# Sums and rounding passes of the ternary weights: in blocks early on, or in twelve steps spread over the head of the program

## The reference

```python
x = _layernorm(x + attn(x))            # 16 heads on 4 KV heads, rotary, ALiBi, softmax
x = _layernorm(x + xattn(x, ctx))      # 16 heads of 16, windows of 64, masks by cell
x = _layernorm(x + ffn(x))

def _weight_quant(w):                  # w_gate, w_up, w_down: 1024 x 256, 1024 x 256, 256 x 1024
    scale = 1.0 / jnp.clip(jnp.mean(jnp.abs(w)), 1e-05)
    return jnp.clip(jnp.round(w * scale), -1.0, 1.0) / scale
gate = silu(bitlinear(x, w_gate)); up = bitlinear(x, w_up)
ffn = bitlinear(gate * up, w_down)     # activations rounded to 8 bits per token
```

## Time and profile before

| | before |
|---|---|
| median of 3 runs | 2233.26 us (2232.71 to 2235.64) |
| the profiled execution | 2231.77 us |
| its span, first to last instruction | 2230.0 us |
| mean granted TensorE clock | 0.999 |
| PE busy | 2155.6 us, 97% |
| DVE busy | 1950.3 us, 87% |
| ACT busy | 1704.1 us, 76% |
| POOL busy | 1424.6 us, 64% |

### The profile page before, as it was taken

The page is one execution under the profiler, slowest core; times in us unless marked ns, Lnnn a source line. Parts: engine busy times, 40 slices in busy tenths (PEclk is TensorE's granted clock), DMA queues, the critical chain, the costliest instruction groups (busy, mean ns, idle before and its releaser), DMA issues. The chain is left out here.

```text
span 2230.0 us, 58875 instructions
## 1 busy us (share of the span) xinstructions
PE 2155.6 (97%) x19819; PEld 1671.1 (75%) x19819; DVE 1950.3 (87%) x7968; ACT 1704.1 (76%) x4754; POOL 1424.6 (64%) x1678
## 2 busy tenths in 40 slices
PE   7899999999999999999999999999999999999987
PEld 6677777777787777777777777777777777777755
DVE  5779988999988899998899998889999888999874
ACT  4687778887778888777888777788877788887743
POOL 2566766666776666776666677666667666667631
PEclk9999999999999999999999999999999999999999
DMA  4010111111110110111111111111011101101100
GB/s 164 11 34 25 37 27 33 28 35 28 36 37 23 34 31 25 37 37 30 30 28 36 26 37 37 25 35 28 25 37 37 38 23 28 37 25 37 32 16 10
DMA packets 85400, 74.69 MB, mean 33 GB/s; under 512 B 18544, under 2 KB 79344, under 8 KB 85104
## 3 DMA queue, kind: packets, MB, share of 16 engines
q1 hardware_dynamic: 85104, 70.93, 11.9%
HBM read 45.72 MB, written 8.39 MB: 24 GB/s over the span
## 5 line engine op out<-in xcount | busy, mean ns | idle before, releaser
L1404 POOL TENSOR_TENSOR prob<-prob,precs 128x512 f32<-128x512 f32 x512 | 528.8, 1040 | 561.8 <-DVE precs L1017 557.6
L1312 ACT ACTIVATE prob<-prob,nmax 128x256 f32<-128x256 f32 x1024 | 509.0, 505 | 45.1 <-DVE nmax L1010 45.1
L1010 DVE CUSTOM_DVE_ANT_0 prob<-bank,alibi 128x256 f32<-128x256 f32 x1024 | 371.2, 418 | 23.4 <-PE bank L728 23.1
L1319 ACT COPY pT<-bank 128x512 f32<-128x512 f32 x512 | 303.4, 593 | 55.8 <-PE bank L617 55.5
L617 PE MATMUL bank<-ident,prob 128*128 128x128 f32 x2048 | 316.6, 277 | 4.0 <-ACT pT L1319 3.0
L1336 ACT ACTIVATE px<-px,nmx 128x128 f32<-128x128 f32 x1024 | 313.9, 400 | 4.8 <-DVE nmx L1119 4.8
L617 PEld LDWEIGHTS bank<-ident,prob 128*128 128x128 f32 x2048 | 231.3, 141 | 56.5 <-issue 38.1
L747 PE MATMUL bank<-pT,v_sb 128*64 128x256 f32 x2048 | 249.8, 386 | 3.4 <-DVE qq_lo L1001 3.1
L1119 DVE CUSTOM_DVE_ANT_0 px<-bank,mask 128x128 f32<-128x128 f32 x1024 | 226.3, 286 | 4.8 <-PE bank L807 3.0
L747 PEld LDWEIGHTS bank<-pT,v_sb 128*64 128x64 f32 x2048 | 136.2, 136 | 100.9 <-issue 39.3
L1312 ACT ACTIVATION_READ_ACCUMULATOR prob<-prob,nmax 128x1 f32 x1024 | 199.5, 195 | 0.0
(11 more groups left out here) (216 smaller groups left out, 6028.9 us busy)
## 6 DMA issues: line engine op xcount, KB each, us to landing
raw<-in_xT SPq DMA_DIRECT2D x32, 256.0 KB, 2.9
xtok<-in_x SPq DMA_DIRECT2D x32, 256.0 KB, 2.9
kx_tok<-in_ctx SPq DMA_DIRECT2D x32, 256.0 KB, 3.0
raw<-in_ctxT SPq DMA_DIRECT2D x32, 256.0 KB, 2.9
kx<-k_sin SPq DMA_DIRECT2D x256, 32.0 KB, 2.0
vs<-vx SPq DMA_DIRECT2D x64, 128.0 KB, 2.3
out_y<-x SPq DMA_DIRECT2D x32, 256.0 KB, 3.1
cellk<-in_cell SPq DMA_DIRECT2D x32, 64.0 KB, 3.8
```

The costliest lines, as they stand in the source:

```text
L1010: v.tensor_tensor_reduce(out=prob[:, (2 * p + q) % SLOTS, c, :], in0=psum[SCORES[c]][:, q * L:(q + 1) * L], in1=alibi[:, p % 2, :], scale= ...
L1312: nc.scalar.activation(prob[:, (2 * p + q) % SLOTS, c, :], prob[:, (2 * p + q) % SLOTS, c, :], ACT.Exp, bias=nmax[:, i:i + 1], scale=-1.0, ...
L1319: nc.scalar.copy(pT[:, p % 2, :, :, q * P:(q + 1) * P].rearrange("p c k n -> p (c k) n"), bank[:].rearrange("p (c n) -> p c n", c=4)).then ...
L1404: g.tensor_tensor(prob[:, n % SLOTS, :, :], prob[:, n % SLOTS, :, :], precs[:, 2 * n:2 * n + 2].unsqueeze(2).to_broadcast([P, 2, L]), ALU. ...
```

## The change

The instructions and their operands stay the same. They move in the lists of `HEAD`. The sums become a step kind of their own, `sum` m on ACT, and the passes a kind `ternary` m, i on DVE, one pass each. The twelve steps stand between steps of batches 0 and 1. The matmul ("prep", 5) moves on PE from behind the last `Q` of batch 0 to behind `S` 6 of batch 0, the mean ("prep", 6) on DVE to the same place. `kx_clear` on POOL moves from between `R` 5 and 6 to between `R` 13 and 14. PE loses 26 fillers, 7 of another 15, and 8 of another 14. A pass waits for the one before it at its start, and only the last of each matrix still waits for its own end. The steps ("prep", 6 to 8) on ACT, which are waits alone, move later, and so does ("prep", 8) on PE. `BODY`, `TAIL` and SP's list are unchanged.

```diff
     "dve": [
-        (0, 'qT', 1), (0, 'Q', 0, 2), (0, 'prep', 6), (0, 'Q', 1, 2), (0, 'S', 2), (0, 'prep', 7), (0, 'qT', 2),
+        (0, 'W', 0), (0, 'ternary', 0, 0), (0, 'R', 12), (0, 'R', 13), (1, 'qT', 0), (0, 'ternary', 0, 1), (0, 'S', 7),
+        (0, 'ternary', 0, 2), (0, 'mask'), (0, 'R', 14), (0, 'R', 15), (0, 'O', 2), (0, 'ternary', 1, 0), (1, 'kT'),
+        (1, 'S', 0), (0, 'ternary', 1, 1), (1, 'qT', 1), (0, 'ternary', 1, 2), (1, 'R', 0), (1, 'R', 1), (1, 'Q', 0, 2),
+        (1, 'S', 1), (0, 'ternary', 2, 0), (1, 'R', 2), (0, 'O', 3), (0, 'ternary', 2, 1), (1, 'S', 2), (0, 'ternary', 2, 2),
...
                     dve.wait_ge(pre_dve, P_CROSSED + 4)
-                    ternary(0)
-                elif n > 6:
-                    ternary(n - 6)
-
-            def ternary(m):
-                done = P_CROSSED + 4 + 3 * m
-                v.tensor_scalar(stage[m], stage[m], wrec[:, m:m + 1], MAGIC, ALU.mult, ALU.add).then_inc(pre_dve, 1)
-                dve.wait_ge(pre_dve, done + 1)
-                v.tensor_scalar(stage[m], stage[m], MAGIC, 1.0, ALU.subtract, ALU.min).then_inc(pre_dve, 1)
-                dve.wait_ge(pre_dve, done + 2)
-                v.tensor_scalar((wg16, wu16, wd16)[m][:].rearrange("p k n -> p (k n)"), stage[m], -1.0, None, ALU.max).then_inc(pre_dve, 1)
-                dve.wait_ge(pre_dve, done + 3)
+
+            def ternary(m, i):
+
+                dve.wait_ge(pre_dve, P_CROSSED + 4 + 3 * m + i)
+                if i == 0:
+                    v.tensor_scalar(stage[m], stage[m], wrec[:, m:m + 1], MAGIC, ALU.mult, ALU.add).then_inc(pre_dve, 1)
+                elif i == 1:
+                    v.tensor_scalar(stage[m], stage[m], MAGIC, 1.0, ALU.subtract, ALU.min).then_inc(pre_dve, 1)
+                else:
+                    v.tensor_scalar((wg16, wu16, wd16)[m][:].rearrange("p k n -> p (k n)"), stage[m], -1.0, None, ALU.max).then_inc(pre_dve, 1)
+                    dve.wait_ge(pre_dve, P_CROSSED + 4 + 3 * m + 3)
...
-                        elif args[0] == 5:
-
-                            act.wait_ge(later_loaded[2], 16 * len(later_loads[2]))
-                            act.wait_ge(wo_split, 2)
-                            for m in range(3):
-                                if m > 0:
-                                    act.wait_ge(w_sums, m)
-                                nc.scalar.activation(kx[:].rearrange("p k h n -> p (k h n)"), stage[m], ACT.Abs, accum_out=wsum[:, m:m + 1])\
-                                    .then_inc(w_sums, 1)
+                    elif kind == "sum":
+
+                        m, = args
+                        act.wait_ge(later_loaded[2], 16 * len(later_loads[2]))
+                        act.wait_ge(wo_split, 2)
+                        if m > 0:
+                            act.wait_ge(w_sums, m)
+                        nc.scalar.activation(kx[:].rearrange("p k h n -> p (k h n)"), stage[m], ACT.Abs, accum_out=wsum[:, m:m + 1]).then_inc(w_sums, 1)
```

## The result

| | before | after |
|---|---|---|
| median | 2233.45 us of 7 runs (2232.71 to 2235.64) | 2244.13 us of 7 runs (2239.83 to 2244.99) |
| the profiled execution, its span | 2231.77, 2230.0 us | 2244.49, 2242.7 us |
| mean granted TensorE clock there | 0.999 | 0.995 |

The ratio is 1.0046, 95% interval 1.0037 to 1.0056: 10.7 us slower. The forecast had the sign, but only half of the size, and the time lies outside its range (up to 2242.5).

What follows compares the result with a forecast made beforehand. PE bounds the kernel, busy 97%, with DVE's list binding in the head. 3.0 us earlier, then 7.7 later, gives 4.75 late; plus 0.7 for clock and 1.5 from profile to median: 2238.7 us, range 2231.5 to 2242.5.

Steps and rivals of the forecast that it cites:

- Part 1: Head up to W 0 of batch 0: passes and sums moved away make it 3.0 us earlier.
- Part 2: From W 0 of batch 0 to qT 2 of batch 1: 7.7 us lost, leaving qT 2 4.75 us late.
- the walk through DVE's list: Stepping through DVE's list from 89 us, nine passes of 1.23 us plus POOL waits: qT 2 of batch 1 4.75 us late.
- the wrong branch: Pass 3 near 95 us gets in ahead of POOL's memsets, ending at 96.05; losing to them would cost another 1.2 us.
- The clock: PE waits 2 us ahead of kT and 3.3 ahead of V of batch 1; a drop costs 0.7 us, at most 1.7.
- Neither stretch can take up a delay: PE from 117 us, and 140 to 165 us where ACT is busy, have no room to absorb lateness.
- a constant shift to the end: From qT 2 of batch 1, near 120 us, lateness stays the same through the rest of the execution.
- the dense part: The stretch where PE waits for next to nothing, from about 186 us, so head gains or losses carry through.
- The 41 fillers cost nothing, apart from the clock: The removed PE fillers in the head stood in waits, so removing them changes no time except through the clock.
- The passes fit: Rival, chance 0.32: passes lose nothing to POOL in part 2; 1.2 us late, 2234.5 us, no difference.
- the lead survives: Rival, chance 0.11: the 3.0 us lead reaches qT 2 of batch 1, kT at 95.5 or earlier; 2228.8 to 2230.3 us.
- Memsets and clock both go wrong: Rival, chance 0.14: pass 3 waits for both memsets, clock falls at kT and V; 7.7 us, 2241.0 us.

Runs made afterwards that it cites:

- e8_again: The changed kernel run once more, unedited: 2242.68 us, ratio to before 1.0047.
- e4_sums_back: The changed kernel with the three sums, their matmul with its 26 fillers, and the mean back in their old places, passes still spread: 2239.78 us, ratio 1.0032.
- e14: e10 without the 12 fillers ahead of SX 0 of batch 0: 2243.23 us, ratio to before 1.0049.
- e10: The changed kernel with fillers in every PE wait over 1.5 us up to 150 us, 271 in the head: 2240.90 us, ratio to before 1.0036.
- e16: e10 with 33 more fillers in PE's waits, 304 in the head: 2237.70 us, ratio to before 1.0024.
- e13: e10 with the kx memsets moved behind R 15 and 14 fillers ahead of kT: 2243.25 us, ratio to before 1.0045.
- e12: The kernel before with only the change's removal of 41 fillers: 2233.28 us, ratio to before 1.0004.
- e18: The kernel before with 47 more fillers in PE waits up to 100 us, 257 in the head: 2240.66 us, ratio to before 1.0040.
- e5: The changed kernel with the first two passes of each weight matrix cut from 2048 to 64 columns: 2234.82 us, ratio to before 1.0011.
- e9: e6 with fillers added in its three waits, ahead of qT 2, qT 0 of batch 1 and SX 0: 2228.94 us, ratio to before 0.9984.
- e15: e9 with one pass less behind O 0 of batch 0, moved ahead of S 6, later passes one place on: 2228.57 us, ratio to before 0.9980.
- e17: The changed kernel with 41 fillers put back in other PE waits ahead of 80 us: 2242.16 us, ratio to before 1.0043.
- e6: The changed kernel with sums, matmul, mean, passes and memsets placed where traces show their engines idle: 2230.65 us, ratio to before 0.9989.
- e2_kx: The changed kernel with the two kx memsets on POOL moved from behind R 13 to behind R 15: 2239.91 us, ratio to before 1.0030.
- e3: The changed kernel with the edits of both e1 and e2_kx: 2238.77 us, ratio to before 1.0029.
- e11: The changed kernel with sums 0 and 1 moved ahead of T 0 and sum 2 behind the split of qT 2: 2239.56 us, ratio to before 1.0028.
- e1: The changed kernel with 28, 24 and 12 fillers ahead of kT and V of batch 1 and SX 0: 2239.52 us, ratio to before 1.0030.
- e7: The changed kernel with the three passes on hh moved to where cross attention of batch 0 ends: 2238.55 us, ratio to before 1.0030.

## Why the prediction was right in sign and wrong in size

**Part 1, 3.0 us earlier: right, as long as the clock is up.** W 0's addition came at 88.44, forecast 88.6. In e8_again, behind two low stretches, the lead was 0.4 us. Spreading the sums was not needed for it: e4_sums_back has the same lead with the sums in the old place. The mean beside W 0 and kx_clear as seen from SP cost nothing, as said: in e14 W 1 and px are equally late.

**Part 2, the walk through DVE's list: right, with the wrong branch taken.** The forecast took the pass ahead of the memsets and kept the other as 1.2 us more. It waited for both: it ended at 97.73, forecast for that branch 97.9; kT stood at 99.78, forecast 99.95. With the clock at 1.00 W 1 is 5.5 us late (e10, e14, e16), where the walk with the memsets gives 4.75 + 1.2 = 6.0. The memsets measured 1.7 to 1.8 us (e13 against e10), not 1.2; the forecast's own two values for kT, 98.1 and 99.95, lie 1.85 apart, so its 1.2 was too little by its own walk. The rule of the Trainium skill ("SBUF — State Buffer", section on the two separate sides) would have given the branch that did not come. The passes that meet the rotations (CS) were forecast to wait 0.1, 1.2 and 1.0 us and took 1.28, 2.27 and 2.17, which is 0.05, 1.0 and 0.9 of waiting.

**The clock, 0.7 us and at most 1.7: this is the step that failed.** The working said "3.4 us at half clock cost at most 1.7 us" and counted one drop. It had named two waits, of 2 and 3.3 us. The first became 3.80 with the memsets, the low clock behind it lasted 6.8 us; the second brought another, and SX 0 a third. Together with the wait at SX 0 they took 5.8 us (px 11.3 against 5.5 in e14), 1.6 of it up to W 1. The wait at SX 0, which the forecast did not have at all, is 1.6 of the 5.8 (2.15 against 0.53), so the low clock alone took 4.2 where the sum had 0.7. The 11.3 us at px are then 3.8 for the walk without the memsets (W 1 in e13; forecast 4.75), 1.7 for the memsets, 4.2 for the clock and 1.6 for SX 0. The medians agree: after or e8_again at 1.0046 to 1.0047 against e16 at 1.0024 are 5 us, and what is left in e16, 0.24% or 5.4 us, is the walk with the memsets and the fillers that e16 has of its own.

**"Neither stretch can take up a delay", "a constant shift to the end": right for the walk, wrong for after.** Delay was not taken up but grew, from 7.1 at W 1 to 11.3 at px, by two low stretches and 1.6 us more at SX 0. With the clock up, e16 stays between 5.5 and 6.6 up to batch 30. The forecast said that a shift that changes after 120 us would speak against the dense part; what it spoke against was the clock term.

**"The 41 fillers cost nothing, apart from the clock": right here by luck.** e12 shows about 1 us, inside the interval. e18 shows that 47 more in waits of the same stretch cost 8.3. And of the fillers taken away, 7 stood ahead of qT 2, where a wait of 1.97 us is left that a low clock follows in some executions.

**The rivals.** The passes fit and the lead survives both fell: e5 shows that two thirds of the cut passes' time lay on the path up to W 1, and kT was at 99.78, not at 95.5. "Memsets and clock both go wrong" is what happened, mechanism and places as written, with 1.7 us for the memsets and 4.2 for the clock where it had 1.2 and 1.7, and SX 0 on top. The low stretches behind its two named waits, 6.8 and 3.4 us, can cost 5.1 us by its own reckoning of half clock (an estimate); a range that allowed this would have held the time.

What stays open: why the early low stretches (61 to 75 us) come in some executions and not in others. None came in the seven traces with 17 or 22 fillers ahead of qT 2 (e9, e10, e13, e14, e15, e16, e17), and after and e8_again, the same program, differ in them. It is also open why e15 lost 1.3 us early in the loop, and what the last batch adds: after, e6, e8, e13, e14 and e18 lose 2.2 to 3.2 us more there, with a low clock somewhere between 2110 and 2127 us, and the others at most 0.7. That the packets of q8 slow the issues is seen in their times; which instructions make a packet come when it does was not tried.

## What to carry to other kernels

In a list that runs strictly in order, a moved step costs what it exceeds the idle gap by in which it lands: put it in gaps that the trace shows, with the other engine idle too, and not evenly. A new wait of some 2 us or more on PE may bring half clock behind it, here for 3.4 to 10 us. Price each such wait with its own low stretch, and repeat runs, since those of one program (e2_kx) span 8 us. A filler that is longer than its wait costs the difference: 12 ahead of SX 0 cost 0.8 us. When only fillers change, compare medians of variants with different counts before believing a difference of 0.2 or 0.3%.

## What the hardware showed unexpectedly

- The wait of 3.79 or 3.80 us ahead of kT was followed by the lower clock level in all six executions that had it, the one of 3.07 to 3.11 ahead of V in five of six (not in e4_sums_back). Waits of 1.97 or 1.98 us ahead of qT 2 were followed by it in e3, e4, e5, e6, e8 and e11, and not in after, e1, e2 and e7. The wait of 2.77 us ahead of O 0 was followed by it in before, the same wait (2.78) in e12 was not. A low stretch lasted from 3.4 to 10 us (e11_sums_gap, 95.4 to 105.6).
- A DVE pass waits for both of two memsets that follow each other on POOL: 3.46 us where 1.69 stood without them (after, e2_kx), and also when it is reached within the first of them (e5_short, 95.33).
- A packet of the instruction queue q8 at 144.5 us, just as the last of eight small transfers was issued, went with a longest landing of 3.6 us in place of 2.1 (after); one among the eight issues went with 5.79 us for them in place of 5.13 (e18). In which batches that happened went with the number of fillers ahead of the loop in all traces but one (e15): 47 fillers more took 8.3 us of the median, 5.8 of it in the trace between W 1 of batch 0 and batch 30 (e18).
